# Graph layers on one core: first-layer table built with x against turned bases, no reorder transfers, half-row stores

## The reference

```python
weight = jnp.einsum('rb,bio->rio', w_comp, bases)   # 32 relations from 8 bases, 256x256 each
xw = jnp.einsum('ni,rio->nro', h, weight)           # [6250, 32, 256]
msg = xw[src, rel_type] * norm
out = jax.ops.segment_sum(msg, dst, num_segments=h.shape[0])
return jax.nn.relu(out)
x = _layernorm(x + _L0_gnn_ref(x, ...), axis=-1)
```

## Time and profile before

| what | us |
|---|---|
| median of 3 runs | 7217.41 |
| span of the profiled execution | 6364.3 |
| time beside the span, by that median | 853.1 |
| `layer0`, from the barrier to the next stage's first DMA issue | 77.18 to 805.29 |
| its first base product, its first table store | 84.51, 105.33 |

### The profile page before, as it was taken

The page is one execution under the profiler, slowest core; times in us unless marked ns, Lnnn a source line. Parts: engine busy times, 40 slices in busy tenths (PEclk is TensorE's granted clock), DMA queues, the critical chain, the costliest instruction groups (busy, mean ns, idle before and its releaser), DMA issues.

```text
span 6364.3 us, 77713 instructions
## 1 busy us (share of the span) xinstructions
PE 4985.1 (78%) x19175; PEld 3374.5 (53%) x19176; DVE 3946.2 (62%) x9442; ACT 1596.1 (25%) x3091; POOL 3597.4 (57%) x3549
## 2 busy tenths in 40 slices
PE   5999869999987777776666666279999997776766
PEld 3555547777773433333444444257787874333333
DVE  5555566666646666666666666876666665655555
ACT  3555534444440000001222222123333331000000
POOL 0000067777757777776777777223333335777776
PEclk8888889999997777777888887679999997667676
DMA  6999956666654444445777777267666774344343
GB/s 231 364 361 365 371 190 216 217 216 217 216 198 122 124 124 124 124 124 154 242 244 244 242 245 245 76 197 237 236 233 234 238 241 139 116 117 116 116 117 111
DMA packets 476381, 1279.57 MB, mean 201 GB/s; under 512 B 137938, under 2 KB 262716, under 8 KB 412533
## 3 DMA queue, kind: packets, MB, share of 16 engines
q1 hardware_dynamic: 315557, 832.27, 37.5%
q0 software_dynamic: 160464, 443.17, 24.2%
HBM read 636.68 MB, written 587.04 MB: 192 GB/s over the span
## 4 chain that ended last, share of the span: by engine, by line
PE 58%; DVE 11%; issue 10%; DMA 9%; POOL 6%; SPq 3%; ACT 1%; DVEq 1%; POOLq 0%; ACTq 0%
PE ps L1409 27%; PE ps L1584 11%; PE ps L1433 8%; PE ps L1567 5%; DMA table<-A 5%; POOL ring L630 3%; POOL A L630 2%; PE ps L1369 2%; DMA work<-place_dram 2%; DVE W L816 2%; DVE A L816 2%; PE ps L1384 1%; SPq L476 1%; SPq L355 1%; DMA A<-gat_table,ix 1%
## 5 line engine op out<-in xcount | busy, mean ns | idle before, releaser
L618 POOL DMA_INDIRECT ring<-table,idx x2490 | 2366.4, 950 | 1640.0 <-DVEq L840 774.8
L1409 PE MATMUL ps<-ring,W 128*128 128x256 f32 x3320 | 1189.5, 476 | 440.4 <-DVE W L816 278.0
L1409 PEld LDWEIGHTS ps<-ring,W 128*128 128x128 f32 x3320 | 683.3, 229 | 869.2 <-DVE W L816 399.6
L816 DVE TENSOR_SCALAR W<-iota,dloc,norm 128x128 f32<-128x128 f32 x1660 | 597.6, 361 | 766.7 <-PE ps L1409 756.8
L1409 PE MATMUL ps<-ring,A 128*128 128x256 f32 x1660 | 724.6, 543 | 271.5 <-DVE A L816 210.8
L643 POOL TENSOR_TENSOR ring<-ring,work 128x1024 f32<-128x1024 f32 x208 | 405.7, 1951 | 809.8 <-DMA ring<-rows_dram 809.8
L1584 PE MATMUL ps<-W_r,work_r 128*128 128x512 f32 x1960 | 701.1, 440 | 0.0
L834 DVE TENSOR_TENSOR X<-X,ps 128x256 f32 x1660 | 688.2, 415 | 17.2 <-PE ps L1409 15.2
L1409 PEld LDWEIGHTS ps<-ring,A 128*128 128x128 f32 x1660 | 340.2, 248 | 620.2 <-DVE A L816 367.6
L1433 PE MATMUL ps<-W_r,work_r 128*128 128x512 f32 x1568 | 560.0, 439 | 0.0
L1148 DVE TENSOR_TENSOR X<-X,ps 128x264 f32 x830 | 352.4, 425 | 329.4 <-PE ps L1567 272.8
(11 more groups left out here) (239 smaller groups left out, 7045.1 us busy)
## 6 DMA issues: line engine op xcount, KB each, us to landing
table<-A SPq DMA_DIRECT2D x294, 1024.0 KB, 6.2
ring<-rows_dram SPq DMA_DIRECT2D x208, 528.0 KB, 4.6
table<-A SPq DMA_DIRECT2D x49, 1280.0 KB, 5.4
table<-W SPq DMA_DIRECT2D x49, 1280.0 KB, 6.9
rows_dram<-ring SPq DMA_DIRECT2D x52, 1056.0 KB, 4.8
rows_dram<-A SPq DMA_DIRECT2D x52, 1056.0 KB, 4.6
ring<-table,idx POOLq DMA_INDIRECT x2490, 2.8
A<-W SPq DMA_DIRECT2D x264, 128.0 KB, 5.3
```

Source lines behind the costliest of these rows:

```text
L618: pool.indirect_dma_start(out=f_ring[:, s % NR, :], out_offset=None, in_=src, in_offset=bass.IndirectOffsetOnAxis(ap=idx[:, s:s + 1], axis ...
L816: return dve.tensor_scalar(marks_[:, k % G, :], iota[:, :], dloc[:, k:k + 1], norm[:, k:k + 1], ALU.is_equal, ALU.mult).then_inc(wk.onehot ...
L1409: pe.matmul(ps[:, s % banks, 0:D], marks_[:, s % G, :], f_ring[:, s % NR, :], start=True, stop=True).then_inc(wk.step_done, 1)
```

## The change

Windows are taken two at a time, in 25 pairs; the last pair has one window that is stored. The bases are now the stationary operand and x of both windows (256 columns) moves. The columns of the bases are put in a new order at the split, so that one base product `m` (8 for each pair) yields, for 32 output columns, all 8 bases on the 128 partitions: 64 partitions for 16 output columns. So the product comes out in the order that the combine wants, and ACT and DVE split it directly from PSUM into `l_high` and `l_low` (three pairs, by `m % 3`). The combine takes these as the stationary operand on 64 rows of the array at a time and moves a 64 x 256 matrix that holds `w_comp` at the right places. Its two banks for each window `w` are copied by ACT (first) and DVE (second), in runs of 8 columns, to the half-row buffers `l_table`: one for each half `t` of the output columns and each `w`. A half is stored in one transfer of 2 MB, in pieces of 512 bytes in DRAM (half of a 1 KB row). The table is in natural order, and `idx` takes one instruction. x is no longer loaded whole in `setup` (6272 KB) but two windows at a time.

```diff
-                load(X[:, 0:NW1, :], x[0:NW1 * P].rearrange("(w p) c -> p w c", p=P))
...
-                for i in range(16):
-                    load(comb_raw[i * BASES:(i + 1) * BASES, i // 4, i % 4 * R0:(i % 4 + 1) * R0], w_compT)
+                for i in range(P // OS):
+                    load(comb_row[i * OS:(i + 1) * OS, :], w_compT[i % BASES].partition_broadcast(OS))
...
+                rows = table.rearrange("(w p) (r t o) -> w t p r o", p=P, r=R0, t=2)
...
+                def load_x(k):
+                    if k >= 2:
+                        sp.wait_ge(l_turned, k - 1)
+                    sp.dma_start(l_x[k % 2], x_rows[k]).then_inc(l_x_in[k % 2], 16)
+
+                def store_half(k, t, w):
+                    m = OQ * k + (t + 1) * OQ // 2 - 1
+                    sp.wait_ge(l_act, banks_before(m, w) + 1)
+                    sp.wait_ge(l_dve, banks_before(m, w) + 1)
+                    sp.dma_start(rows[2 * k + w, t], l_table[2 * t + w]).then_inc(l_t_free[2 * t + w], 16)
...
+                def low_xb(m):
+                    dve.wait_ge(xb_high, m + 1)
+                    dve.tensor_tensor(l_low[m % 3], base_bank(m).rearrange("p (h n) -> p h n", h=2), l_high[m % 3].bitcast(F32),
+                                      ALU.subtract).then_inc(xb_low, 1)
...
+                def to_table(m, w):
+                    k, q = m // OQ, m % OQ
+                    if q % (OQ // 2) == 0 and k >= 1:
+                        dve.wait_ge(l_t_free[2 * (q // (OQ // 2)) + w], 16 * k)
+                    dve.wait_ge(l_full, 2 * banks_before(m, w) + 2)
+                    dve.tensor_copy(table_place(m, w, 1), comb_bank(w, 1).rearrange("p (h r o) -> p h r o", h=2, o=OS)).then_inc(l_dve, 1)
...
+                def base_products(m):
+                    k, q = m // OQ, m % OQ
+                    if q == 0:
+                        pe.wait_ge(x_low, k + 1)
+                    if m >= 3:
+                        pe.wait_ge(xb_low, m - 2)
+                    terms = [(b_high, l_xt_high, c) for c in range(2)] + [(b_low, l_xt_high, c) for c in range(2)] + [(b_high, l_xt_low, c) for c in range(2)]
+                    for h in range(2):
+                        for n, (w, rows, c) in enumerate(terms):
+                            ins = pe.matmul(base_bank(m)[:, h * 2 * P:(h + 1) * 2 * P], w[:, c, q, h, :], rows[k % 2][:, c, :],
+                                            start=(n == 0), stop=(n == len(terms) - 1))
...
+                def combine(m, w):
+                    if w == 0:
+                        pe.wait_ge(xb_low, m + 1)
+                    if m >= 1:
+                        pe.wait_ge(l_act, banks_before(m - 1, w) + 1)
+                        pe.wait_ge(l_dve, banks_before(m - 1, w) + 1)
+                    terms = [(l_high, comb_high), (l_low, comb_high), (l_high, comb_low)]
+                    for h in range(2):
+                        for n, (rows, c) in enumerate(terms):
+                            for s in range(2):
+                                part_ = slice(s * 64, (s + 1) * 64)
+                                ins = pe.matmul(comb_bank(w, s)[:, h * CC:(h + 1) * CC], rows[m % 3][part_, h, w * P:(w + 1) * P], c[part_, :],
+                                                start=(n == 0), stop=(n == 2))
```

More of the change, by code:

```diff
@@ L127, in build @@
[L127 to L132, removed]
+        OS = 8
@@ new lines, in build @@
+        l_x = [XF[:, u * 512:(u + 1) * 512].rearrange("p (w c) -> p w c", w=2) for u in range(2)]
+        comb_raw = targets1[:, 0:CC]
+        comb_row = targets1[:, CC:CC + R0]
+        comb_place = targets1[:, CC + R0:CC + R0 + OS]
+        l_xt_high, l_xt_low = ([work_r[:, (2 * v + u) * 512:(2 * v + u + 1) * 512].rearrange("p (c n) -> p c n", c=2) for u in range(2)] for v in range(2))
+        assert BASES * 2 * OS == P and 3 * half <= 2 * NSC and 4 * BW + half <= 2 * NSC and 3584 <= U * GROW and 2 * CC == 512
@@ L243, in build, with blocks_of, banks_before @@
         z_zero, z_ps = sem("z_zero"), sem("z_ps")
[L246 to L249, removed]
+        (b_split_high, b_split_low, c_made, c_high, c_low, l_turned, x_high, x_low, l_xb_full, xb_high, xb_low, l_full, l_act,
+         l_dve) = (sem("l_" + n) for n in ("b_high", "b_low", "c_made", "c_high", "c_low", "turned", "xt_high", "xt_low", "xb_full", "xb_high",
+                                           "xb_low", "full", "act", "dve"))
+        l_x_in = [sem(f"l_x_in{u}") for u in range(2)]
         l_t_free = [sem(f"l_t_free{h}") for h in range(4)]
+        def blocks_of(k):
+            return min(2, NW1 - 2 * k)
+        def banks_before(m, w):
+            k = m // OQ
+            return OQ * sum(blocks_of(i) for i in range(k)) + (m % OQ) * blocks_of(k) + w
         class Walk:
@@ L343, in layer0_transfers @@
             def layer0_transfers(_):
[L344 to L369, removed]
@@ L373, in head_loads @@
+                load_x(0)
+                load_x(1)
+                for k in range(NSB):
+                    for t in range(2):
+                        for w in range(blocks_of(k)):
+                            store_half(k, t, w)
+                    if k + 2 < NSB:
+                        load_x(k + 2)
+                for t in range(2):
+                    for w in range(2):
+                        sp.wait_ge(l_t_free[2 * t + w], 16 * sum(blocks_of(k) > w for k in range(NSB)))
             def head_loads():
@@ L1171, in layer0_copies @@
             def layer0_copies(_):
[L1172 to L1179, removed]
-                    act.wait_ge(l_xb_full, XBANKS * k + b + 1)
-                    act.activation(l_xb[:, b * 512:(b + 1) * 512], ps[:, 1 + b % 2, :], ACT.Copy).then_inc(l_xb_free, 1)
@@ new lines, in layer0_copies @@
+                high_x(0)
+                act.wait_ge(b_split_low, 8)
+                for m in range(AHEAD):
+                    high_xb(m)
+                for m in range(OQ * NSB):
+                    k, q = m // OQ, m % OQ
+                    if m + AHEAD < OQ * NSB:
+                        high_xb(m + AHEAD)
+                    for w in range(blocks_of(k)):
+                        to_table(m, w)
+                    if q == OQ // 2 and k + 1 < NSB:
+                        high_x(k + 1)
@@ new lines, in layer0_products @@
+                turn_x(0)
+                pe.wait_ge(b_split_low, 8)
+                pe.wait_ge(c_low, 1)
+                for m in range(AHEAD):
+                    base_products(m)
+                for m in range(OQ * NSB):
+                    k, q = m // OQ, m % OQ
+                    if m + AHEAD < OQ * NSB:
+                        base_products(m + AHEAD)
+                    for w in range(blocks_of(k)):
+                        combine(m, w)
+                    if q == OQ // 2 - 1 and k + 1 < NSB:
+                        turn_x(k + 1)
```

210 lines of the change are left out of this document (83 added, 127 removed).

## The result

| | before | after |
|---|---|---|
| median, us | 7218.94 (4 runs, 7214.42 to 7223.92) | 7349.49 (4 runs, 7342.05 to 7353.9) |
| first base product / first table store | 84.51 / 105.33 | 84.57 / 102.47 |
| next stage's first DMA issue | 805.29 | 932.33 |

The kernel is slower by 130.5 us, ratio 1.0178 with a 95% interval of [1.0164, 1.0192], outside the forecast range of 7185 to 7300. The span of the changed kernel's profile is 7340.2 us. The first layer accounts for 932.33 - 805.29 = 127.0 of the 130.5.

The account below looks back on a forecast made before the run. Transfers bound the first layer: first store at 100.0, stores and x 716.4, end 1.9 give 818.3 against 805.3, 13 us more; added to the median, 7230 us. Eight-in-ten range 7185 to 7300, the forecast's own 7210 to 7258.

Parts of the forecast that it names:

- SP stands in its queue behind each store's wait with only the load of x behind it, which is two pairs early: First layer, SP's queue: only the load of x follows the waiting stores, two pairs early; no time was added for it.
- the rival in which PE is slow: First layer: weight loads or the 64-row form cost more, deciding from 3.6 us per m; at 3.8, 7274 us; chance 12%.
- The queue does not run dry: First layer's DMA queue: about 8 us of work precede a half's next store while two queued stores take 14.2 us.
- The term of pieces: First layer's stores: 27.8 ns per 512-byte piece, 7.12 us per half-row store, 697.5 us for 98 stores.
- the line: Piece cost fitted through 8 KB stores and 1 KB loads: 9.5 ns plus 36.8 ns per 1000 bytes, 28.4 ns at 512.
- The page's rule: Store pieces: about 3 fabric cycles fixed per packet, so 22.4 ns for 512 bytes and transfers no longer bind.
- Setup and the head of the layer: Before the first store: gathers end 3 us sooner without x's load, barrier at 74.2, first store at 100.0 us.
- PE's product: First layer on PE: base product 1.65 us plus two combines 1.70 us, 3.35 us for each m.
- Two products ahead: First layer on PE: three banks and two base products ahead cost nothing and hide the splits.
- The direction, slower: Whole kernel: chances were slower 0.48, same 0.35, faster 0.17.
- PE becomes the bound: First layer: pieces under 26.0 ns leave PE binding at 27.4 us a pair, 32 us less, 7185 us; chance 17%.
- Pieces cost more than the line: First layer's stores: pieces cost more, deciding from 28 ns; at 30.5 ns, 81 us more in all, 7298 us; chance 12%.

Follow-up runs that it names:

- x early: Changed kernel with the load of x for pair k + 2 issued ahead of pair k's four stores on SP: 7191.59 us, ratio 1.0042.
- the one with whole rows: Changed kernel with x loaded ahead of stores, three whole-window buffers, 16 KB store runs in natural order, second window four products behind: 7112.18 us, ratio 0.9931.

## Why the prediction was wrong

**The step that failed** is "SP stands in its queue behind each store's wait with only the load of x behind it, which is two pairs early". The load is two pairs ahead by its number, and not by time. It stands behind all four stores of pair k, so it can't be issued before pair k's last copy, and PE turns that x with product 4 of pair k + 1, about 12 us later: 390.3 for the copy's end, when SP takes the last store, 402.1 for PE's stop (407.57 less 5.5). In these 12 us SP issues the last half store for 5.5, and the load then needs 11.6, with two stores of 2 MB, 14 us of transfer, issued just ahead of it: its pieces pass behind theirs, as the packets above show. The prediction added up what the queue has to carry and asked whether it runs dry; it never followed the load of x from its issue to its use. Its cost is shown by moving that line: 96.7 us of the layer. Against PE's own period of 26.5 us (x early, contiguous stores) the 33.8 seen are 7.3 more: 5.5 of wait, 1.4 in the product at the fallen clock (4.67 - 3.24) and 0.4 in the turn of x there. Moving the load gives back 4.0 of them, 33.8 to 29.8, because the transfers bind from there on.

**The clock's share.** The rows of before had shown 1.2 GHz in part of the layer after pauses, and the prediction used that only for the rival in which PE is slow. The stretches above show it here: granted 0.56 in 407 to 413, right after the wait, mostly the lower level of 1.2 GHz, and 1.00 in 417 to 427. A wait of 5.5 us once for each pair costs its length and 1.8 us more. The waits of 1.2 us in the run with contiguous stores and the late load did not cost this: the same stretch there was granted 1.00.

```profile
407.00:413.00 6.00, 5.32 (x54) 4.92 (x54) 2.22 (x4) 2.28 (x4) 0.00 (x0) 1.00 1.03 435
```

**"The queue does not run dry"** fell with it: the DMA share is 0.60 in 417 to 427. With the load moved it holds, at 1.04 in 106 to 800.

**The term of pieces was mis-sized by a little.** 512-byte pieces were taken at 27.8 ns; at 290 GB/s over 16 engines they take 16 x 512 / 290 = 28.2, and the line had 28.4. The choice to shade the line down, because its 1 KB row stood at a share of 108%, was wrong: the stores too queue above 100% (104%). With x early the layer lasts 733.2 us, where the prediction had 718.3; 98 x 256 x 0.4 ns = 10 of these 15 us would be the piece. But 28.2 counts x's 1 KB pieces like the stores'. If the load of x is taken out of the 29.8 us of a pair with the prediction's 0.76, 28.4 ns are left for a store's piece, as the line had, and that is all of the 15. The traces here do not tell the two apart. The working with all terms: 2.5 us from a later first store, 14.9 from this, and 97 from the late load are 114 us over the forecast's 818.3, and that gives the 932.3 seen. Some 5 us more up to 7349.5 are the 3.5 that lie behind the layer and the 1.5 by which the median of before moved with its fourth run.

**The page's rule.** The Trainium skill (DMA: Bandwidth & Descriptors, "Why small descriptors are slow (HBM only)") gives about 3 fabric cycles of fixed cost for a packet, from which the prediction estimated 22.4 ns for 512 bytes and a layer bound by PE. The trace with x early does not agree: 28.2 ns. The estimate by the rule is 6 ns low here as it was for 1 KB and 8 KB, so the difference seen in the earlier trace rows carries over unchanged to the smaller piece.

**Setup and the head of the layer.** The saving was put at 3 us with bounds 0 and 4. The last gather landed at 37.7 us and not 38.6, so taking x out of `setup` freed about 1 us there, and the layer begins at 75.7, where the chain of before had 77.2 and the forecast 74.2. From there to the first base product it takes 8.8 us and not the 7.5 forecast. So that product came at 84.57, where 81.7 was forecast: half of the miss is in each of the two terms.

```profile
30.15 7.57 DMA W<-in_edges,stat
75.77 0.92 SPq L361 DMA_DIRECT2D X<-in_x  x2
84.57 6.08 PE L1383 MATMUL ps<-work_r,W_r 128*128 128x256 f32 x36 [4.82 <-DVE work_r L762]
```

**What was right.** PE's product: 1.62 us for 12 base matmuls and 1.62 for 24 combine matmuls, 3.24 in all, against 3.35; weight loads hide behind 256 columns, and 64-row pairs cost nothing of their own. DVE's and ACT's copies in runs of 8 columns take 682 and 599 ns, where whole ones took 685 and 596. Two products ahead gained nothing where one was tried in its place. The direction, slower, had been given 0.48; the step that took the time out of the range was in no rival. Of the rivals, "PE becomes the bound" is wrong for this kernel, and right for the one with whole rows, which saves 51.5 us of the way to the next stage (804.28 to 752.74, on two chips) where the rival, by its slower product, had 32. "PE slower" is refuted by 3.24 us. "Pieces cost more than the line" is too, by 28.2 to 28.4 ns against 28.4; but the prediction had let this rival decide from 28 ns and its own forecast run to 28.9, so by these bounds the measured piece lies in both.

## What to carry to other kernels

How early a load is counts in time between its issue and its use, not in iterations: follow each one through its own queue, with what waits and what still transfers ahead of it there, above all on a queue that also holds stores. A load without a dependency on this iteration's work goes ahead of the waits for it. A transfer's pieces are priced from at least two rows of the same trace as a fixed part and a part by size, without shading; and cutting a store in two halves of a row can give back all that a removed reorder had saved: 733.2 us with x early, against 699.3 before.

## What the runs showed of the hardware

- A 512-byte piece of a store costs 28.2 to 28.4 ns on one of 16 engines, at 290 GB/s, some 9.6 ns of it for being a piece (480 added pieces in 4.6 us); whole 8 KB pieces moved at 421 GB/s.
- The issue of a transfer on SP takes longer the more pieces are queued ahead of it. A 2 MB store in 4096 pieces took 0.54 us when it came alone (389.68 above) and 5.4 to 5.5 right behind another in the rows above; the load of only 256 KB behind both took 6.0 to 8.8 over the layer. With stores in 16 KB pieces the second store took 0.33, and the load behind it 1.2 for most pairs and 2.7 in the row above. All that stands behind such an issue on SP is late by it.
- A load of 256 KB behind two stores of 2 MB in one queue lands when they are through, 11.6 to 12.7 us after its issue. Two kernels' landing times and the order of the packets in one say so; no run changed the number of stores ahead of it.
- TensorE's granted clock was at 0.56 in the six microseconds after a wait of 5.5 us, and at 1.00 after one of 1.2.
- The same kernel differs by 0.8% between chips (7218.94 and 7161.32 us), and one profiled execution had a span some 800 us shorter than another of the same kernel, behind the first layer; the cause of that is open.
